# Which spectrum is copied: reordering one period of a four-layer kernel

## The chip, the cores and the metric

The kernel runs on one core of a Trainium2 chip. TensorE (PE) multiplies matrices into PSUM, VectorE (DVE), ScalarE (ACT) and GpSimd (POOL) do elementwise work, SyncE (SP) issues all DMAs. Each engine runs its own list of instructions in order and waits at semaphores. The metric is the device time of one execution in microseconds.

## The reference, cut to what matters

```
x = x + autocorrelation(layernorm(x), ctx, ctx)      # (32, 128, 1024), 8 heads
x = x + base(layernorm(x)) + experts(layernorm(x))   # 1024x1024 base, 8 LoRA experts, top 2
x = x + window_attention(layernorm(x), ctx)          # 8 heads, window 16
x = x + experts4(x)                                  # 4 LoRA experts, top 2

# autocorrelation, per batch, along the 128 rows of each of 1024 columns:
corr = ifft(fft(q) * conj(fft(k))).real ; k = v = ctx
w, idx = top_k(corr, 9) ; w = softmax(w)
out[t] = sum_i w_i * v[min(idx_i + t, 127)]
```

All of it is f32. The correlation is a product of two spectra. The transforms of 128 rows are products with tables of cosines and sines.

## The kernel before, in words

The 32 batches are independent. Each passes through three groups of stages: *a* (layer norm, spectra, correlation, top 9, softmax, aggregation by spectra, first residual), *b* (second norm, router, base product, experts, second residual, third norm, keys, values and queries) and *c* (window attention and last experts). Every engine runs a software pipeline: one step is one period, and in it up to four batches have their stages interleaved by hand in a function `step(i, live)`, where `live(lag)` says whether batch i - lag exists. All order is in these lists and in the semaphores; nothing is planned at run time. A full step has all stages.

PSUM is held by three tensors: `pa` (four banks of 512 f32; `pa_lo` is banks 0 and 1, `pa_hi` banks 2 and 3) for the a-stages and the projections of the context, `pb` (two) for the b-stages, `pc` (two) for the c-stages.

What the change touches, in the order of one period:
- `a_products` (L1105, DVE): four products of the weights' spectra with the context's long spectra `v_re`, `v_im`. Two of them read `pa_lo`, two `pa_hi`. `a_sum` (L1422 and L1424, POOL) adds them into `agg_re`, `agg_im`, one half of the columns after the other, four sums.
- `b_queries`: TensorE makes the attention's queries in `pb`, ACT writes their high half (L864), DVE the low half (L1149, output `sc`). `b_query_blocks` (L877 on ACT, L1450 on POOL) spreads the queries by head into `q_diag`, in two halves of eight blocks, six by ACT and two by POOL.
- `b_values(b, odd)` (L1169, DVE): transposes the values; SyncE then places them with four DMAs (L439, output `v_diag`).
- `gates` (L1180 to L1209, DVE): softmax and scaling of the experts. `c_mid` transposes the result (L696), `experts_mid` copies it on ACT, `c_delta` multiplies (L703, L704), `c_result` adds (L1261, DVE).
- `a_aggregate` (L561, L563): the inverse transform, in `pa` banks 0 and 1. `a_residual` (L1115, DVE) adds x, one half after the other, into `x_b`; `b_norm` (L1021) takes batch norm statistics of both halves; `variance` (L1025); POOL's `root` (L1395, L1400); `b_norm_rows` (L1038) writes the normalised rows `xn_b`, which `rows_to_features` (L575) transposes into `pb`.
- `a_context` (L495 to L497) transforms the next batch's context into `pa_lo`, `a_query` (L486) its query into `pa_hi`. `a_values` (ACT, L777) copies the context's spectrum from `pa_lo` to SBUF: first the two 64-row halves crosswise (real part to the imaginary rows) into `v_im`, then all into `v_re`. `a_product` (L1060, L1062, DVE) multiplies the query's spectrum in `pa_hi` with both. `a_corr` (L523, L524) transforms the products back, into banks 0 and 1. `a_context_long(b, n)` transforms the context in double length into `pa_hi`, real part (n = 0), then imaginary (n = 1), and `a_values_long` (ACT) copies these to `v_re` and `v_im`. The second waits for the first copy.
- `c_scores(b, g)` on PE (L649 to L657) makes one of four groups of attention scores in `pc`; on DVE `c_scores` takes their maximum (L1219) and `c_subtract` subtracts it (L1229). PE's next group waits for that subtraction. ACT's `c_exp` (L897), DVE's `c_sums` (L1236, L1238), POOL's `c_normalise` (L1458), ACT's `c_high` and POOL's `c_low` (L1431) follow.

The next period begins on PE with `b_router` (L591).

## Time and profile before

| | |
|---|---|
| time, median of 3 runs | 1823.69 us (1823.42 to 1826.07) |
| profiled execution | 1823.51 us, span 1821.7 us |
| busy, share of the span | PE 94%, DVE 86%, ACT 62%, POOL 50% |
| chain that ended last | PE 56%, DVE 20%, ACT 10%, POOL 8%, issue 5% |
| granted clock of PE, mean | 0.976 |
| one of ACT's query blocks (L877) | 710 ns, 384 of them |
| DMAs that place the values | 128 KB each, 5.0 us from issue to landing |

The clock is given as a share of full speed, 2.4 GHz. A busy PE is not a PE at its peak, since matmuls overlap in the pipeline and their ends are modelled: what a matmul costs is the distance between two starts. Idle time of an engine that is not the bottleneck costs nothing by itself.

### The profile page before, as it was taken

The numbers are of one execution on the slowest core, as the hardware profiler recorded it, in microseconds if no ns is written. First come the engines' busy times: TensorE is split into PE (matmuls) and PEld (weight loads), VectorE is DVE, ScalarE is ACT, GpSimd is POOL, SyncE is SP. The second block draws the span as 40 slices with busy tenths as digits, with TensorE's granted clock in tenths as the row PEclk, the third lists the DMA queues.
The fourth block names the chain that finished last, engine by engine and source line by source line (L and its number), as shares of the span: only waits on it lengthen the run. The fifth ranks groups of instructions, "written<-read, shape, count | busy, mean of one in ns | idle before, by whom it ended". The sixth has DMA issues, their size and how long they took to land.

```text
span 1821.7 us, 48202 instructions
## 1 busy us (share of the span) xinstructions
PE 1704.5 (94%) x19296; PEld 1081.3 (59%) x19296; DVE 1571.8 (86%) x4758; ACT 1131.7 (62%) x1929; POOL 903.1 (50%) x933
## 2 busy tenths in 40 slices
PE   4699999999999999999999999999999999999975
PEld 2356566666656666655666665666665666666553
DVE  7779889889889888988988898988898998889853
ACT  5257656666765666665666676566666666657642
POOL 2355554555554545555455555444555545555432
PEclk8899999999999999999999999999999999999995
DMA  6033322243332233332223343223443322333220
GB/s 225 24 59 71 59 53 51 52 71 71 71 59 48 50 58 71 71 66 48 51 50 71 71 71 59 50 50 55 71 71 71 47 49 50 69 71 59 31 30 24
DMA packets 549359, 111.37 MB, mean 61 GB/s; under 512 B 531088, under 2 KB 531344, under 8 KB 548624
## 3 DMA queue, kind: packets, MB, share of 16 engines
q1 hardware_dynamic: 549136, 108.30, 31.8%
q8 instruction: 152, 2.49, 0.6%
q14 instruction: 71, 0.58, 0.1%
HBM read 57.94 MB, written 16.78 MB: 41 GB/s over the span
## 4 chain that ended last, share of the span: by engine, by line
PE 56%; DVE 20%; ACT 10%; POOL 8%; issue 5%; DMA 0%; DVEq 0%; SPq 0%; POOLq 0%; ACTq 0%
PE pb L602 18%; PE pc L677 8%; ACT q_diag L877 6%; POOL prob L1424 4%; POOL rest L1422 4%; PE pa L523 4%; ACT v_im L777 3%; PE pa L495 3%; PE pa L524 3%; PE pa L496 3%; PE pa L497 3%; PE pb L591 3%; DVE rows_c L1251 2%; PE pa L563 2%; DVE rest L1105 2%
## 5 line engine op out<-in xcount | busy, mean ns | idle before, releaser
L602 PE MATMUL pb<-w_base_h,even_words 128*128 128x512 f16 x1024 | 324.8, 379 | 0.0
L1431 POOL TENSOR_TENSOR p_hl<-sc,p_hl 128x512 f16<-128x512 f32 x128 | 164.1, 1282 | 219.9 <-ACT p_hl L777 219.9
L1458 POOL TENSOR_TENSOR sc<-sc,sc_rec 128x512 f32<-128x512 f32 x128 | 134.4, 1050 | 266.2 <-DVE sc_rec L1238 266.2
L877 ACT ACTIVATE q_diag<-sc,own 128x512 f32<-128x512 f32 x384 | 244.3, 710 | 3.1 <-DVE sc L1149 3.1
L602 PE MATMUL pb<-w_base_l,even_words 128*128 128x512 f16 x512 | 193.9, 379 | 0.0
L486 PE MATMUL pa<-xn_a,tab 128*128 128x512 f32 x384 | 180.7, 607 | 3.8 <-ACT xn_a L777 3.8
L677 PEld LDWEIGHTS pc<-sc_t,v_diag 128*128 128x128 f16 x6144 | 170.2, 97 | 20.6 <-DVE sc_t L1245 5.9
L677 PE MATMUL pc<-sc_t,v_diag 128*128 128x32 f16 x6144 | 173.9, 177 | 5.5 <-DVE sc_t L1245 5.5
L655 PE MATMUL pc<-k_h,q_diag 128*128 128x32 f16 x2048 | 169.0, 177 | 0.0
L656 PE MATMUL pc<-k_l,q_diag 128*128 128x32 f16 x2048 | 168.4, 177 | 0.0
L657 PE MATMUL pc<-k_h,q_diag 128*128 128x32 f16 x2048 | 168.4, 177 | 0.0
L656 PEld LDWEIGHTS pc<-k_l,q_diag 128*128 128x128 f16 x2048 | 158.7, 97 | 15.8 <-issue 1.1
L602 PEld LDWEIGHTS pb<-w_base_h,even_words 128*128 128x128 f16 x1024 | 99.9, 98 | 113.7
L655 PEld LDWEIGHTS pc<-k_h,q_diag 128*128 128x128 f16 x2048 | 161.1, 97 | 7.9
L657 PEld LDWEIGHTS pc<-k_h,q_diag 128*128 128x128 f16 x2048 | 158.3, 97 | 0.0
L777 ACT ACTIVATE v_im<-pa 64x1024 f32<-64x1024 f32 (+1 forms) x96 | 98.1, 1021 | 95.8 <-PE pa L497 94.2
L777 ACT ACTIVATE rows_c<-pc 64x256 f32<-64x256 f32 x256 | 96.4, 376 | 95.1 <-PE pc L677 92.0
L1219 DVE TENSOR_REDUCE sc_max<-pc 128x16 f32<-128x512 f32 x128 | 84.5, 660 | 74.3 <-PE pc L657 74.3
L777 ACT ACTIVATE p_hl<-sc 128x512 f16<-128x512 f32 x128 | 100.7, 787 | 55.4 <-POOL sc L1458 51.0
L495 PE MATMUL pa<-ctx_hl,w_ctx_h 128*128 128x512 f16 x320 | 121.4, 379 | 12.5 <-POOL ctx_hl L1416 10.7
L1450 POOL TENSOR_TENSOR q_diag<-sc,own 128x512 f32<-128x512 f32 x128 | 129.2, 1042 | 5.5 <-DVE sc L1149 5.5
L1422 POOL TENSOR_TENSOR rest<-rest,v_im 128x512 f32<-128x512 f32 x64 | 81.8, 1279 | 90.8 <-DVE v_im L1105 90.8
(165 smaller groups left out, 4658.4 us busy)
## 6 DMA issues: line engine op xcount, KB each, us to landing
x_a<-in_x SPq DMA_DIRECT2D x32, 512.0 KB, 5.8
x_res<-in_ctx_in SPq DMA_DIRECT2D x32, 512.0 KB, 5.6
x_res<-in_x SPq DMA_DIRECT2D x32, 512.0 KB, 3.7
v_diag<-even_words SPq DMA_DIRECT2D x128, 128.0 KB, 4.9
v_diag<-p_hl SPq DMA_DIRECT2D x128, 128.0 KB, 5.0
out<-rows_c SPq DMA_DIRECT2D x32, 512.0 KB, 2.6
v_diag<-in_base_w SPq DMA_DIRECT2D x4, 1024.0 KB, 10.1
q_diag<-in_ra SPq DMA_DIRECT2D x1, 544.0 KB, 13.8
```

The costliest lines, as they stand in the source:

```text
L486: last = mm(place[:, n + h, :], lhsT, moving[:, h * HALF:(h + 1) * HALF], start=True, stop=True)
L495: mm(pa[:, n + h, :], w_ctx_h[:, table, :], high[:, cols], start=True, stop=False)
L602: mm(pb[:, h, :], rows[:, cols], weights[:, j, h * HALF:(h + 1) * HALF], start=(j == 0 and m == 0), stop=False)
L655: mm(place, q_halves[:, blk, :, HI], k_h[:, keys], start=False, stop=False)
L656: mm(place, q_halves[:, blk, :, HI], k_l[:, keys], start=False, stop=False)
L657: last = mm(place, q_halves[:, blk, :, LO], k_h[:, keys], start=False, stop=(i == GB - 1))
L677: last = mm(place, v_halves[:, blk % 2 * NBLK // 2 + blk // 2, :, v_part], p_halves[:, g % 2, i, :, p_part], start=(m == 0), stop=(m == 2))
L777: return nc.scalar.activation(dst, src, ACT.Copy)
L877: nc.scalar.activation(q_diag[:, blocks, head * QB:(head + 1) * QB], q_hl.rearrange("p (n t) -> p n t", t=QB)[:, blocks], ACT.Copy, scale= ...
L1422: g_.tensor_tensor(agg_re[:, cols], agg_re[:, cols], v_im[:, cols], ALU.add).then_inc(sum_w.sem, 1)
L1431: g_.tensor_tensor(part[:, :, :, LO], sc[:, g % 2, :, :], part[:, :, :, HI], ALU.subtract)\
L1458: g_.tensor_tensor(sc[:, g % 2, :, :], sc[:, g % 2, :, :], sc_rec[:, blocks].unsqueeze(2).to_broadcast([P, GB, KEYS]), ALU.mult)\
```

## The change

Of the two spectra that are multiplied, ACT now copies the query's (`a_query_crossed`, `a_query_same`), and DVE reads the context's from PSUM. The product comes out with the sign of its imaginary part turned, so one table changes its sign. PE makes the query's spectrum ahead of the aggregation, and the first long context directly behind the context, since `pa_hi` is free when ACT has copied it. The transposes of the second norm come before the first group of scores, and each half of the correlation comes behind a group of scores. On DVE the statistics of each half of the first residual directly follow that half (each waits for it), the product comes ahead of the first group's maximum and subtraction, and the queries' low half ahead of the values' second transpose. On ACT the copies move ahead of most query blocks.

```diff
-    corr_2 = np.concatenate([sin, -sin])
+    corr_2 = np.concatenate([-sin, sin])
@@ PE, a_context_long(b, 0)
-                    pe.wait_ge(prod_q.sem, prod_q.after(b))
-                    pe.wait_ge(prod_q2.sem, prod_q2.after(b))
+                    pe.wait_ge(v_out.sem, v_out.after(b))
@@ PE, step
                     c_router(i - 3)
+                if live(0):
+                    a_query(i)
                 if live(1):
                     a_aggregate(i - 1, 0)
...
                 if live(0):
                     a_context(i)
+                    a_context_long(i, 0)
+                if live(1):
+                    rows_to_features(i - 1, 0, 1, xn_b, pb)
                 if live(2):
                     c_scores(i - 2, 0)
                 if live(0):
-                    a_query(i)
-                if live(1):
-                    rows_to_features(i - 1, 0, 1, xn_b, pb)
+                    a_corr(i, 0)
                 if live(2):
                     c_scores(i - 2, 1)
                 if live(0):
-                    a_corr(i, 0)
-                    a_context_long(i, 0)
                     a_corr(i, 1)
@@ ACT
-            def a_values(b):
-                act.wait_ge(mm_ctx.sem, mm_ctx.after(b))
+            def a_query_crossed(b):
+                act.wait_ge(mm_q.sem, mm_q.after(b))
                 if not first(b):
                     act.wait_ge(sum_w.sem, sum_w.after(b - 1, 3))
                 for half in range(2):
...
-                    copy(v_im[rows, :], pa_lo[other, :]).then_inc(v_out.sem, 1)
+                    copy(v_im[rows, :], pa[other, 2:4, :].rearrange("p n t -> p (n t)")).then_inc(v_out.sem, 1)
+            def a_query_same(b):
+                act.wait_ge(mm_q.sem, mm_q.after(b))
                 if not first(b):
                     act.wait_ge(sum_w.sem, sum_w.after(b - 1))
-                copy(v_re[:, :], pa_lo).then_inc(v_out.sem, 1)
+                copy(v_re[:, :], pa_hi).then_inc(v_out.sem, 1)
@@ ACT, step
                     b_queries(i - 2)
-                if live(3):
-                    experts_exp(i - 3, 1, pc, E1)
-                if live(2):
                     b_query_blocks(i - 2, 0, 0)
                     b_query_blocks(i - 2, 5, 0)
+                if live(3):
+                    experts_exp(i - 3, 1, pc, E1)
+                if live(0):
+                    a_query_crossed(i)
+                if live(3):
+                    experts_mid(i - 3, 1)
+                if live(0):
+                    a_query_same(i)
+                if live(2):
                     b_query_blocks(i - 2, 1, 0)
-                if live(3):
-                    experts_mid(i - 3, 1)
...
-                if live(0):
-                    a_values(i)
@@ DVE, a_product
-                dve.wait_ge(mm_q.sem, mm_q.after(b))
+                dve.wait_ge(mm_ctx.sem, mm_ctx.after(b))
...
-                v.tensor_tensor(c2, pa_hi, v_im[:, :], ALU.mult).then_inc(prod_q2.sem, 1)
+                v.tensor_tensor(c2, pa_lo, v_im[:, :], ALU.mult).then_inc(prod_q2.sem, 1)
...
-                v.tensor_tensor(c1[:, :], pa_hi, v_re[:, :], ALU.mult).then_inc(prod_q.sem, 1)
+                v.tensor_tensor(c1[:, :], pa_lo, v_re[:, :], ALU.mult).then_inc(prod_q.sem, 1)
@@ DVE, a_residual, after each half
+                    dve.wait_ge(x1_out.sem, x1_out.after(b, h + 1))
+                    v.bn_stats(bn[1][:, h, :], x_b[:, cols]).then_inc(ln_bn[1].sem, 1)
@@ DVE, step
                 if live(1):
+                    b_queries(i - 1)
                     b_values(i - 1, 1)
-                    b_queries(i - 1)
                 if live(2):
                     gates(i - 2, 1, pc, E1)
                 if live(0):
                     a_residual(i)
+                    variance(i, 1)
                 if live(2):
                     c_result(i - 2, 0)
                 if live(0):
-                    b_norm(i, 1, x1_out)
-                    variance(i, 1)
-                if live(1):
-                    c_scores(i - 1, 0)
-                if live(0):
                     b_norm_rows(i, 1)
-                if live(1):
-                    c_subtract(i - 1, 0)
                 if live(-1):
                     a_product(i + 1)
+                if live(1):
+                    c_scores(i - 1, 0)
+                if live(1):
+                    c_subtract(i - 1, 0)
                 if live(2):
                     c_result(i - 2, 1)
```

## Rows read from the trace of the kernel before

**Rows 1.** Windows: busy us and (xrecords) per engine, clock, DMA share, GB/s.
```profile
754.90:808.60 53.70, 52.44 (x604) 33.41 (x603) 48.14 (x149) 34.88 (x61) 27.91 (x30) 1.00 0.34 60
```

**Rows 2.** Timeline of PE: start, length, engine, line, what, xcount, [idle before <-releaser].
```profile
796.12 3.60 PE L486 MATMUL pa<-xn_a,tab 128*128 128x512 f32 x8
...
804.81 1.07 PE L561 MATMUL pa<-rest,tab 128*128 128x512 f32 x2
...
808.77 0.22 PE L696 MATMUL pc<-ident_h,mid_hl 128*128 128x128 f16 x1
...
809.36 0.39 PE L703 MATMUL pc<-w_b_hh,mid_t 128*128 128x512 f16 x1 [0.37 <-ACT mid_t L777]
...
811.53 0.38 PE L649 MATMUL pc<-band_bf,ident_bf 128*128 128x512 bf16 x1
...
812.96 1.96 PE L486 MATMUL pa<-xn_a,tab 128*128 128x512 f32 x4
...
814.76 1.04 PE L575 MATMUL pb<-ident,xn_b 128*128 128x128 f32 x8
...
815.63 0.38 PE L649 MATMUL pc<-band_bf,ident_bf 128*128 128x512 bf16 x1
...
817.56 0.49 PE L523 MATMUL pa<-tab,xn_a 128*128 128x128 f32 x2 [0.35 <-DVE xn_a L1062]
...
823.96 0.38 PE L495 MATMUL pa<-ctx_hl,w_ctx_h 128*128 128x512 f16 x1
...
825.25 0.22 PE L591 MATMUL pb<-w_ra_h,even_words 128*128 128x136 f16 x1
```

**Rows 3.** Timeline of DVE, the same period.
```profile
803.75 1.24 DVE L1169 STREAM_TRANSPOSE p_hl<-v_pad 128x1024 f32<-128x1024 f32 x1
...
804.91 1.34 DVE L1149 SCALAR_TENSOR_TENSOR sc<-pb,bias_att,sc 128x1024 f16<-128x1024 f32 x1
...
806.14 0.14 DVE L1180 TENSOR_SCALAR small<-pc 128x4 f32<-128x4 f32 x1
...
808.22 1.45 DVE L1115 TENSOR_TENSOR x_b<-pa,x_res 128x512 f32<-128x512 f32 x2
...
811.04 1.28 DVE L1021 BATCH_NORM_STATS2 small<-x_b 128x6 f32<-128x512 f32 x2
...
812.36 0.20 DVE L1025 BATCH_NORM_AGGREGATE small<-small 128x2 f32<-128x12 f32 x1
...
813.76 0.80 DVE L1038 TENSOR_SCALAR xn_b<-x_b,small 128x1024 f32<-128x1024 f32 x1
...
819.39 0.63 DVE L1219 TENSOR_REDUCE sc_max<-pc 128x16 f32<-128x512 f32 x1
...
820.05 0.69 DVE L1229 TENSOR_TENSOR sc<-pc,sc_max 128x512 f32<-128x512 f32 x1
...
833.38 0.69 DVE L1219 TENSOR_REDUCE sc_max<-pc 128x16 f32<-128x512 f32 x1 [1.59 <-PE pc L657]
```

**Rows 4.** Timeline of ACT, POOL and the SyncE queue, the same period.
```profile
803.29 1.43 ACT L864 ACTIVATE sc<-pb,bias_att 128x1024 f16<-128x1024 f32 x1
...
805.01 5.74 SPq L439 DMA_DIRECT2D v_diag<-p_hl  x4
...
806.49 1.26 POOL L1424 TENSOR_TENSOR prob<-prob,v_re 128x512 f32<-128x512 f32 x1
...
812.92 0.55 POOL L1400 TENSOR_TENSOR small<-small 128x1 f32<-128x1 f32 x1
...
817.85 0.62 ACT L897 ACTIVATE sc<-sc 128x512 f32<-128x512 f32 x1
...
821.85 1.02 ACT L777 ACTIVATE v_re<-pa 128x1024 f32<-128x1024 f32 x1
```

**Rows 5.** Timeline, first batch and the end.
```profile
11.74 1.24 ACT L784 ACTIVATE xn_a<-x_a,small 128x1024 f32<-128x1024 f32 x1 [3.44 <-POOL small L1404]
...
1771.87 0.29 PE L696 MATMUL pc<-ident_h,mid_hl 128*128 128x128 f16 x1 [3.23 <-DVE mid_hl L1209]
```

More of the change, by code:

```diff
@@ L986, in step @@
                     b_queries(i - 2)
+                    b_query_blocks(i - 2, 0, 0)
+                    b_query_blocks(i - 2, 5, 0)
                 if live(3):
                     experts_exp(i - 3, 1, pc, E1)
-                if live(2):
-                    b_query_blocks(i - 2, 0, 0)
-                    b_query_blocks(i - 2, 5, 0)
-                    b_query_blocks(i - 2, 1, 0)
+                if live(0):
+                    a_query_crossed(i)
                 if live(3):
                     experts_mid(i - 3, 1)
+                if live(0):
+                    a_query_same(i)
                 if live(2):
+                    b_query_blocks(i - 2, 1, 0)
                     b_query_blocks(i - 2, 3, 0)
@@ L1001, in step @@
                     b_query_blocks(i - 2, 2, 1)
-                if live(0):
-                    a_values(i)
-                if live(2):
                     b_query_blocks(i - 2, 4, 1)
@@ L1115, in a_residual @@
                     v.tensor_tensor(x_b[:, cols], pa[:, h, :], x_res[:, cols], ALU.add).then_inc(x1_out.sem, 1)
-            def b_norm(b, n, before):
-                dve.wait_ge(before.sem, before.after(b))
-                layer_norm(b, n, x_b)
+                    dve.wait_ge(x1_out.sem, x1_out.after(b, h + 1))
+                    v.bn_stats(bn[1][:, h, :], x_b[:, cols]).then_inc(ln_bn[1].sem, 1)
             def b_norm_rows(b, n):
@@ L1340, in step @@
                 if live(0):
-                    b_norm(i, 1, x1_out)
-                    variance(i, 1)
+                    b_norm_rows(i, 1)
+                if live(-1):
+                    a_product(i + 1)
                 if live(1):
                     c_scores(i - 1, 0)
-                if live(0):
-                    b_norm_rows(i, 1)
                 if live(1):
                     c_subtract(i - 1, 0)
-                if live(-1):
-                    a_product(i + 1)
                 if live(2):
```

## The prediction, made before the changed kernel ran

> **What bounds the kernel now.** I read the windows first. In the steady stretch one period, that is one batch, takes 53.70 us and TensorE is busy for 52.44 of it, VectorE for 48.14, ScalarE for 34.88 and GpSimd for 27.91, with TensorE granted its full 2.4 GHz [rows 1]. So TensorE's order of work is the bound, and a change of order can give back only stalls. They are found by going through one period of its timeline and comparing start with start. A row's duration reaches about 0.17 us into the next row when nothing waits (814.76 + 1.04 against 815.63; so the eight f32 records from 796.12, 3.60 long, cost 3.43), so a gap of 0.35 before a row costs about 0.5. From the aggregation's first product (804.81) to the next period's router (825.25) are 20.44 us [rows 2], and the change reorders just this stretch. Three stalls lie in it:
> - the four aggregation products start at 804.81 and the next row at 808.77: 3.96 us, where eight such records cost 3.43. So 0.53 are waits for GpSimd's sums, the last of which ends at 807.75 [rows 2, 4];
> - 808.77 to 809.36, 0.59 us: transpose of the experts' rows, copy by ScalarE, products [rows 2];
> - the correlation starts at 817.56 with 0.35 idle in front of it, released by VectorE's second spectral product: about 0.5 us [rows 2].
>
> The other stalls (transposes of the last norm, the second router) lie ahead of 804.81, and the change leaves them as they are.
>
> **The change, part by part.** Times below are those of the period shown, with 804.81 as the fixed point.
>
> *TensorE.* The query's transform moves in front of the aggregation. It needs all four spectral products of the batch before, the last of which ended when the transpose behind it could start (803.75 [rows 3]), and its rows, made several us earlier. TensorE comes at 804.81: no wait. Now the sum of TensorE alone: query 1.80 (812.96 to 814.76), aggregation 3.43, transpose and copy 0.59, experts' products and context 2.17 (809.36 to 811.53), long context 1.29 (823.96 to 825.25), transposes 0.87 (814.76 to 815.63), scores 1.43 (811.53 to 812.96). That is 11.58, so the first half of the correlation is due at 816.39. The stretch 817.56 to 823.96 (6.40) holds two correlation halves, a long context and scores, so both halves take 6.40 - 1.29 - 1.43 = 3.68. Behind 816.39 come the two halves and two groups of scores, 3.68 + 2.86 = 6.54, which makes the second long context due at 822.93, and its 1.29 bring the next router to 824.22 [rows 2]. Against 825.25 that is 1.03 us less per batch, if nothing else waits. The two stalls that go are covered by the query (sums end 807.75, the aggregation's last product is due at 809.2) and by earlier products on VectorE. The 0.59 stays: transpose and copy remain neighbours.
>
> *VectorE.* This decides whether the due times hold. The low half of the queries now comes before the second transpose of the values. Its source is ScalarE's copy, which ends at 804.72 [rows 4], so VectorE, free at 803.84, stands still for 0.9 us that the transpose hid. I allow 0.05 for a hand-over between engines. Low half at 804.77 (lasts to the next start 1.23: 804.91 to 806.14), transpose at 806.00 (1.16: 803.75 to 804.91), gates at 807.16 [rows 3]. The gates take 2.08 to the first residual half, which I read as the residual's start 808.22 behind 806.14; that puts it at 809.24, against aggregation halves done by about 808.4 and 810.2. Then the halves: a statistics pair without a wait lasts 1.28 for two, 0.60 from start to start; with a wait on the instruction in front the next starts 0.03 after its end (819.39, 0.63 long, next 820.05) [rows 3]. So residual 809.24, statistics 809.96, residual 810.57, statistics 811.29, aggregate 812.01. The two new waits cost about 0.1 each on VectorE, some 6 us over 30 batches were they on TensorE's path. The Trainium skill has a rule here ("VectorE: DVE Perf Modes", section "The DRAIN you can't avoid"): a semaphore after each instruction adds nothing, since the pipe empties anyhow. The trace does not agree: 0.60 without a wait, 0.66 and more with one. By the rule everything from the aggregate on would come 0.2 earlier, the sum would stay what it is (the next lines show TensorE's own order as the later of the two), and only the chance of late hand-offs would shrink. I go by the rows.
>
> From the aggregate's start (812.36) to the end of GpSimd's root (813.47) are 1.11, and 0.06 more to the next start [rows 3, 4]. The norm of the rows therefore starts at 813.18 and ends at 813.98 (0.80). The transposes are due at 804.81 + 9.28 = 814.09: a margin of 0.1. From the norm's start (813.76) to the correlation's (817.56) were 3.80, with a subtraction of 0.67 between; without it 3.13. The correlation is released at 816.31 and due at 816.39, so this stall goes, by a margin of 0.1 again. The second residual half ends at 811.26, and the context products that wait for it are due at 804.81 + 1.80 + 3.43 + 0.59 + 0.88 = 811.51. The gates, done at 809.3, are in time for the experts' transpose at 810.04. Three margins of 0.1 to 0.2 in a row: this is where I may be wrong, and each 0.1 us lost costs 29 x 0.1 = 2.9 us.
>
> *ScalarE.* It copies the query's spectrum instead of the context's: three copies as before, at the 1.02 of the one at 821.85 [rows 4]. The first two now stand before the experts' copy: with the two query blocks (0.71 each) and the small exponential ahead they run from about 808.0 to 810.1; the experts' transpose ends at 810.2. Covered, by 0.1. Were they later, the experts' copy, the products, the context and the residual of the next group stand behind them. The third copy is done by 811.5, before the long context (due 812.8) that now waits for it instead of for the products. The query blocks come about 1.1 us behind their old time and the scores' start moves from 811.53 to 814.96, so they are covered.
>
> *What is late next.* The first scores end at 816.39. I allow 0.19 for the tail of 0.17 and the hand-over, so VectorE's maximum starts at 816.58; subtraction 0.66 later, done at 817.93; ScalarE's exponential at 817.98 against 817.85. From that exponential's start to the end of the copy of the long context (822.87) were 5.02 us of sums, normalising, splitting and copying [rows 4]. It ends at 823.00, TensorE starts at 823.05 and was due at 822.93: a new wait of 0.12. It had 1.1 us of slack before. The third scores need the second subtraction, done at about 821.2 and due at 821.5.
>
> *The moved DMAs.* The values' second transpose ends at 807.24 instead of 804.99, so SyncE's four placements, issued over 5.74 us from 805.01 [rows 4], start 2.3 later, and the load of the context and the store queue behind them. The last one is issued at 811.6 and at the page's 5.0 us lands at 816.6. The first that waits for it is ScalarE's feature copy right behind the exponential, at 818.5; TensorE wants the values at 825. Hidden, with 2 us left. The context load starts at 813, needed at 840.
>
> *Start and end.* In the first batch the query's rows are ready at 12.98, [rows 5]; until then TensorE made the context's transform, and ScalarE copied it during the query's. Now the query goes first and the context follows it: query at 13.0, slowly (at start 1.8 to 3.4 us), context to about 17.4, products to 19.8, long context before the correlation: between 0 and 2 us later, I take 1.2. At the end there is no a-part to hide behind: the gates come a transpose (1.24) later and the experts' transpose at 1771.87 already waited 3.23 for them [rows 5]: 0 to 2.5, I take 1.2.
>
> *Sum.* 1.03 - 0.12 = 0.91 us per batch. 29 steps have all stages: 26.4 us. Start and end give back 2.4. The profiled execution took 1823.51 us (span 1821.7), so 1823.5 - 26.4 + 2.4 = 1799.5. It lies 0.2 under the median of the runs, which changes nothing: 1800.
>
> **The rivals.**
> - *Late hand-offs.* One or more of the margins (norm before transposes, products before correlation, copies before the experts' copy) is missed by a total of 0.4 us. For: three margins near 0.1. Against: the period repeats to 0.02 us in the windows. It gives 1.03 - 0.52 = 0.5 per batch: 1823.5 - 14.5 + 2.4 = 1811.
> - *The gain comes back.* TensorE reaches the second long context early, but the chain of exponential, sums and copy is 0.9 later than I worked out, so that the wait there grows to the full gain. For: the copy is the last link of eight over four engines. Against: each link's time is in the trace. 1823.5 + 2.4 - 0 to 5: about 1823.
> - *VectorE becomes the bound: slower.* It is 0.46 late at the second subtraction (820.51 against 820.05) and TensorE wants its results 0.91 earlier. The only large idle time behind is 1.59 before the fourth maximum [rows 3], so 0.22 are left there; behind it the keys' low half has 0.5 more before TensorE waits. If VectorE is 0.75 us later than I have it, the gain shrinks one for one; from 0.75 + 0.91 = 1.66 on the kernel is slower. At 2.0: 29 x 0.34 + 2.4 = 12, so 1836. For: it is busy 90% and the change adds 0.9 idle and two waits. Against: the sum above leaves those 0.75.
> - *Everything fits and the ends cost nothing:* the whole 1.03 per batch is kept and start and end give nothing back: 1823.5 - 29.9 = 1794. If the query in its new place costs half of 3.43 and not 1.80, 2.6 less.
>
> **How the numbers follow.** Forecast 0.55 (1795 to 1806), late hand-offs 0.22 (1806 to 1818), gain comes back 0.07, slower 0.06, all fits 0.10. The range 1791 to 1816 leaves out the two bad cases, the end of the second and some of the last. A difference of 0.2%, 3.6 us, is about what the measurement can tell: faster than 1820 gets 0.87, within it 0.07, slower 0.06.
>
> **What would show it.** The period from batch to batch falls from 53.70 to about 52.8. The aggregation's products stand 3.43 apart in sum, with no wait for GpSimd. The 0.35 in front of the correlation is gone. VectorE shows a new idle of 0.9 before the queries' low half, released by ScalarE, and less than 0.5 instead of 1.59 before the fourth maximum. TensorE shows a new short wait for ScalarE's copy before the second long context. The 0.37 before the experts' products stays. I am wrong if the transposes wait for the norm by more than 0.2, if the experts' transpose or copy is late, or if the fourth maximum no longer waits for TensorE at all.

## The result, and the profile after

| | before | after |
|---|---|---|
| median of the runs, us | 1824.28 (4 runs) | 1809.38 (4 runs) |
| span of the profiled execution, us | 1821.7 | 1807.6 |
| one period in the steady stretch, us | 53.73 | 53.10 |
| TensorE's clock, mean | 0.976 | 0.975 |

The ratio of the times is 0.9918 (95% interval 0.9903 to 0.9933; brackets behind a ratio hold that interval from here on): faster, by 15 us, inside the range and 9 above the forecast of 1800. Most of what the prediction said is there: the two stalls are gone, the new wait is there at its size. But the period gained 0.63 and not 0.91, and the end cost more than it was given.

The page of the kernel after first, the chain that ended last:

```profile
PE 77%; DVE 15%; issue 4%; ACT 2%; POOL 1%; DMA 0%; DVEq 0%; SPq 0%; POOLq 0%; ACTq 0%
```

TensorE's busy time fell by 5 us only (1704.5 to 1699.1); it is waits that went. The chain runs over TensorE for 77% of the span, before for 56%.

One period of the kernel before, from one router's start to the next, and one of the kernel after, from one query transform to the next:

```profile
771.52:825.25 53.73, 52.47 (x604) 33.41 (x603) 48.17 (x149) 34.91 (x60) 27.94 (x29) 1.00 0.34 61
744.15:797.25 53.10, 52.28 (x606) 33.42 (x605) 48.47 (x149) 34.97 (x60) 27.91 (x30) 1.00 0.31 59
```

The 53.70 of [rows 1], which the prediction took for the period, was the length of a window, 0.03 short of a period. From start to start the kernel before has 53.73. A length taken between two starts of the same instruction does not have this fault.

TensorE's timeline of that period of the kernel after (answers to [rows 2]; a time of before less 60.66 is the same point here):

```profile
744.15 1.93 PE L486 MATMUL pa<-xn_a,tab 128*128 128x512 f32 x4
745.92 1.02 PE L560 MATMUL pa<-rest,tab 128*128 128x512 f32 x2
...
749.35 0.22 PE L695 MATMUL pc<-ident_h,mid_hl 128*128 128x128 f16 x1
749.94 0.39 PE L702 MATMUL pc<-w_b_hh,mid_t 128*128 128x512 f16 x1 [0.37 <-ACT mid_t L777]
...
750.81 0.38 PE L495 MATMUL pa<-ctx_hl,w_ctx_h 128*128 128x512 f16 x1
...
753.42 1.09 PE L574 MATMUL pb<-ident,xn_b 128*128 128x128 f32 x8
754.35 0.38 PE L648 MATMUL pc<-band_bf,ident_bf 128*128 128x512 bf16 x1
...
755.79 0.47 PE L523 MATMUL pa<-tab,xn_a 128*128 128x128 f32 x2
...
757.65 0.38 PE L648 MATMUL pc<-band_bf,ident_bf 128*128 128x512 bf16 x1
...
760.95 0.38 PE L648 MATMUL pc<-band_bf,ident_bf 128*128 128x512 bf16 x1
...
762.50 0.39 PE L495 MATMUL pa<-ctx_hl,w_ctx_h 128*128 128x512 f16 x1
...
763.95 0.23 PE L590 MATMUL pb<-w_ra_h,even_words 128*128 128x136 f16 x1
```

Read it start to start. The aggregation costs 749.35 - 745.92 = 3.43, the price of eight records without a wait. The correlation at 755.79 has nothing idle ahead of it. The experts' wait of 0.37 stands as it did. From the query to the router are 19.80 us; the prediction had 19.53, the kernel before 20.44 from its aggregation, which stood first there, to the router [rows 2]. These 0.64 are the whole gain of the period.

VectorE and ScalarE (answer to [rows 3, 4]):

```profile
744.10 1.38 DVE L1149 SCALAR_TENSOR_TENSOR sc<-pb,bias_att,sc 128x1024 f16<-128x1024 f32 x1 [0.92 <-ACT sc L867]
...
748.58 0.68 DVE L1118 TENSOR_TENSOR x_b<-pa,x_res 128x512 f32<-128x512 f32 x1
749.29 0.69 DVE L1120 BATCH_NORM_STATS2 small<-x_b 128x6 f32<-128x512 f32 x1
749.90 0.67 DVE L1118 TENSOR_TENSOR x_b<-pa,x_res 128x512 f32<-128x512 f32 x1
...
752.56 0.81 DVE L1041 TENSOR_SCALAR xn_b<-x_b,small 128x1024 f32<-128x1024 f32 x1 [0.45 <-POOL small L1398]
...
763.21 0.68 DVE L1133 TENSOR_TENSOR even_words<-pb,even_words 128x512 f16<-128x512 f32 x1
...
772.08 0.69 DVE L1219 TENSOR_REDUCE sc_max<-pc 128x16 f32<-128x512 f32 x1 [0.35 <-PE pc L656]
```

```profile
747.37 2.06 ACT L777 ACTIVATE v_im<-pa 64x1024 f32<-64x1024 f32 x2
749.61 0.28 ACT L777 ACTIVATE mid_t<-pc 128x128 f16<-128x128 f16 x1 [0.18 <-PE pc L695]
...
757.43 0.63 ACT L900 ACTIVATE sc<-sc 128x512 f32<-128x512 f32 x1 [0.51 <-DVE sc L1229]
```

The predicted times hold closely (predicted less 60.66 in brackets): queries' low half 744.10 (744.11), first residual 748.58 (748.58), norm 752.56 (752.52), exponential 757.43 (757.32). The last row of VectorE's fence but one is what the prediction did not look at: the low half of the features ends at 763.89, and the router starts 0.06 later. In the kernel before, the same work ended 1.3 ahead of the router at 825.25:

```profile
823.26 0.68 DVE L1133 TENSOR_TENSOR even_words<-pb,even_words 128x512 f16<-128x512 f32 x1
```

### The profile page after: what moved, and what is told of

Its sections match the earlier page's. It is cut to its first block, busy times and chain, and to the rows that moved or that the text cites. A ratio compares the mean times of both kernels' runs of the same rounds, so it can differ in the third digit from the quotient of the medians.

```text
span 1807.6 us, 48201 instructions
## 1 busy us (share of the span) xinstructions
PE 1699.1 (94%) x19296; PEld 1081.0 (60%) x19296; DVE 1581.0 (87%) x4758; ACT 1132.9 (63%) x1929; POOL 902.3 (50%) x933
## 4 chain that ended last, share of the span: by engine, by line
PE 77%; DVE 15%; issue 4%; ACT 2%; POOL 1%; DMA 0%; DVEq 0%; SPq 0%; POOLq 0%; ACTq 0%
PE pb L601 18%; PE pc L676 8%; PE pa L495 4%; PE pa L496 4%; PE pa L497 4%; PE pa L523 3%; PE pc L689 3%; PE pa L486 3%; PE pa L524 3%; PE pa L562 3%; PE pa L560 3%; PE pb L590 3%; PE pc L655 3%; PE pc L656 3%; PE pc L654 3%
## 5 line engine op out<-in xcount | busy, mean ns | idle before, releaser
L486 PEld LDWEIGHTS pa<-xn_a,tab 128*128 128x128 f32 x384 | 72.4, 196 | 105.9 <-issue 91.3
```

The costliest lines, as they stand in the source:

```text
L486: last = mm(place[:, n + h, :], lhsT, moving[:, h * HALF:(h + 1) * HALF], start=True, stop=True)
```

## Experiments

Each was run beside the kernel before; the medians are those of 4 runs, in experiment 3 of 5. An experiment without another word starts from the kernel after. Three dots in a diff stand for lines left out.

**1. Both halves of the features together.** Is it that row that holds the router?

```diff
                 if live(0):
                     b_features(i, 0)
+                    b_features(i, 1)
                 if live(-1):
                     a_top(i + 1, 0)
-                if live(0):
-                    b_features(i, 1)
```

> The changed kernel with one move on VectorE: the low part of the second half of the features comes directly behind the first half, ahead of the first group of top values. My theory (the router now waits for this low part, 0.16 us in each period, a wait that the prediction had missed): the router follows the long context after 1.29 instead of 1.45, period 52.94, 4 to 5 us less, about 1805. Rival (VectorE's lateness only shows there and is handed on to the next wait): the wait turns up before the attention products or the fourth maximum and the time stays at 1809.

1805.37 us, ratio 0.9895 [0.9881, 0.9908]. Its TensorE and VectorE:

```profile
760.76 0.39 PE L495 MATMUL pa<-ctx_hl,w_ctx_h 128*128 128x512 f16 x1
...
762.07 0.22 PE L590 MATMUL pb<-w_ra_h,even_words 128*128 128x136 f16 x1
```

```profile
758.87 1.28 DVE L1133 TENSOR_TENSOR even_words<-pb,even_words 128x512 f16<-128x512 f32 x2
```

The low half is done at 760.15, 1.9 ahead of the router, and the long context costs 1.31 instead of 1.45 (1.29 in the kernel before). The missed wait is worth 4.0 us of the kernel's time. The rival, by which VectorE's lateness would show up at the next wait and the time stay at 1809, falls.

**2. The values' transpose in its old place on VectorE.** Does the early low half of the queries, with its 0.92 of idle time, hold anything?

```diff
                 if live(1):
-                    b_queries(i - 1)
                     b_values(i - 1, 1)
+                    b_queries(i - 1)
```

> The changed kernel with one swap undone: on VectorE the values' second transpose again comes before the queries' low half. My theory (TensorE's own order is the later of the two up to the correlation): VectorE loses its new 0.92 us of idle, but the first residual half then waits for the aggregation, the norm comes only about 0.3 earlier, and the maximum behind it still waits for the first scores. Only the 0.06 in front of the transposes goes: period 53.0 to 53.1, time 1807 to 1810, at most 2 us under the changed kernel. Rival (VectorE's standstill of 0.92 is what is missing later at the router): the wait at the router goes as well, period 52.9, about 1804.

1807.82 us, ratio 0.9909 [0.9895, 0.9922]: 1.6 us less than after. Its runs lie between 1806.97 and 1809.52 and those of the kernel after between 1809.03 and 1809.99, so the time alone does not show the difference; the period does, with 53.02 for 53.10. The router's wait is unchanged (1.45 from long context to router). VectorE's wait has only moved, into the gates:

```profile
747.18 0.16 DVE L1192 SCALAR_TENSOR_TENSOR small<-small,pc 128x4 f32<-128x4 f32 x1 [0.91 <-ACT pc L887]
```

In the new place the queries are early enough for ScalarE's blocks; in the old one the gates wait 0.91 for the small exponential that ScalarE does behind those blocks. So the residual, at 748.31 with the query at 744.11, comes only 0.23 earlier. The transposes of the norm then cost 0.87, where they cost 0.93 in the kernel after. That 0.06 is the first of the three margins, used up: in the kernel after the norm ended at 753.37, and the transposes were due at 753.41.

**3. Statistics behind both halves of the residual.** What is the part with the statistics worth by itself?

```diff
-                    dve.wait_ge(x1_out.sem, x1_out.after(b, h + 1))
-                    v.bn_stats(bn[1][:, h, :], x_b[:, cols]).then_inc(ln_bn[1].sem, 1)
...
+                dve.wait_ge(x1_out.sem, x1_out.after(b))
+                layer_norm(b, 1, x_b)
```

> The changed kernel with the statistics again behind both halves of the residual. My theory (interleaving fills the wait for the second aggregation half): the aggregate comes 0.28 us later on VectorE, the transposes of the norm then wait 0.2 to 0.3 us, 29 times, and the time rises by 6 to 8 us to 1816. Rival (the two added waits cost what the place gains): no change, 1809.

1817.93 us, ratio 0.9965 [0.9952, 0.9979]: 8.6 us slower than after. Here the query starts at 747.63.

```profile
753.04 0.69 DVE L1118 TENSOR_TENSOR x_b<-pa,x_res 128x512 f32<-128x512 f32 x1 [0.30 <-PE pa L562]
...
756.30 0.81 DVE L1041 TENSOR_SCALAR xn_b<-x_b,small 128x1024 f32<-128x1024 f32 x1 [0.45 <-POOL small L1398]
```

The norm starts 8.67 behind the query, against 752.56 - 744.15 = 8.41, and TensorE takes 3.75 instead of 3.48 from the experts' first product to the transposes: 0.27 for 0.26, one for one. With statistics between the halves, VectorE works in the time in which it now waits 0.30 for the aggregation. Nothing was left of the margin of 0.1 in the prediction, or a part of the 0.26 would have cost nothing.

**4. The query ahead of the aggregation, nothing else** (from the kernel before). Is TensorE's order enough?

```diff
                 if live(0):
-                    a_query(i)
...
+                if live(0):
+                    a_query(i)
                 if live(1):
                     a_aggregate(i - 1, 0)
```

> The kernel before with only the query's transform moved ahead of the aggregation on TensorE. ScalarE still copies the context's spectrum late and VectorE multiplies late. My theory (the correlation's start was tied to the chain of ScalarE's copies and the products): the 0.53 us of waits in the aggregation go, but TensorE then stands 0.9 instead of 0.35 us before the correlation; the period stays 53.7, time 1822 to 1826. Rival (each stall is TensorE's own, so that covering one is a gain): 29 x 0.53 = 15 us less, 1808.

1870.73 us, ratio 1.0252 [1.0238, 1.0266]. Neither theory had it: 1822 to 1826 was expected. TensorE of one period, whose query starts at 774.93:

```profile
780.13 0.22 PE L696 MATMUL pc<-ident_h,mid_hl 128*128 128x128 f16 x1
...
785.98 1.09 PE L575 MATMUL pb<-ident,xn_b 128*128 128x128 f32 x8 [1.50 <-DVE xn_b L1038]
...
788.92 0.49 PE L523 MATMUL pa<-tab,xn_a 128*128 128x128 f32 x2 [0.43 <-DVE xn_a L1062]
```

The aggregation's waits do go: 780.13 - 774.93 = 5.20, the query and eight records. But the query's old place had hidden the norm: the scores in front of the transposes take 3.09 instead of 1.43. The period is 54.97, so 29 of them cost 36 of the 46 us. Of the rest, 9 us were lost by the second router (135.84, in the kernel before 126.67), and no run names their cause. I read this first as a matter of the norm's lateness, and tested that twice.

**5. The same, with the norm of the rows ahead of the maximum on VectorE.**

```diff
                 if live(0):
                     b_norm(i, 1, x1_out)
                     variance(i, 1)
-                if live(1):
-                    c_scores(i - 1, 0)
                 if live(0):
                     b_norm_rows(i, 1)
+                if live(1):
+                    c_scores(i - 1, 0)
```

> The kernel before with the query's transform ahead of the aggregation, and on VectorE the norm of the rows ahead of the first scores' maximum. With the query moved alone the time rose by 46 us: TensorE came to the transposes 1.8 us earlier, while the norm waited behind a maximum that waits for the first scores, and 1.5 us of idle opened there. My theory: that queue on VectorE is the whole loss, and with the norm first the correlation is tied to ScalarE's copies and the products as before, so the period returns to 53.6 to 53.8 and the time to 1820 to 1827, no gain. Rival (with both covers the aggregation's 0.53 us is gained at last): 1808. Second rival (the norm is late for other reasons too): above 1835.

1932.50 us, ratio 1.0589 [1.0574, 1.0605]. VectorE of one period, then two windows inside that period, then two whole periods from router to router, then TensorE:

```profile
807.33 0.81 DVE L1038 TENSOR_SCALAR xn_b<-x_b,small 128x1024 f32<-128x1024 f32 x1 [1.01 <-POOL small L1400]
```

```profile
808.00:810.00 2.00, 1.57 (x11) 1.07 (x12) 1.97 (x4) 1.98 (x3) 1.78 (x1) 0.85 0.38 154
810.00:812.00 2.00, 1.63 (x50) 1.52 (x49) 2.00 (x3) 2.00 (x4) 0.59 (x1) 0.50 0.00 0
```

```profile
650.70:708.60 57.90, 54.91 (x604) 35.52 (x603) 48.40 (x150) 34.92 (x60) 27.93 (x29) 0.94 0.31 56
708.60:764.04 55.44, 52.40 (x605) 33.61 (x604) 47.53 (x146) 34.80 (x60) 27.10 (x29) 1.00 0.33 58
```

```profile
808.19 1.09 PE L575 MATMUL pb<-ident,xn_b 128*128 128x128 f32 x8 [1.33 <-DVE xn_b L1038]
...
811.78 0.80 PE L523 MATMUL pa<-tab,xn_a 128*128 128x128 f32 x2 [0.37 <-DVE xn_a L1062]
...
815.36 0.63 PE L495 MATMUL pa<-ctx_hl,w_ctx_h 128*128 128x512 f16 x1
```

The wait for the norm is nearly as long as in experiment 4 (1.33 for 1.50). VectorE now stands still 1.01 for the root: the statistics start only at 804.80, behind the experts' result, and that waits 0.77 for its products. So the order of norm and maximum was not what held it; what is left is the place of the statistics, which experiment 6 moves.

The 62 us on top of experiment 4 have two parts. The smaller is order: VectorE's products now stand behind norm, maximum and subtraction, and the correlation comes 811.78 - 802.53 = 9.25 behind the experts' transpose, 0.46 later than in experiment 4 (8.79). In a period whose clock stays at 1.00 that is all: 55.44 against 54.97, or some 13 us in 29 periods. The larger is the clock granted to TensorE. It falls to 0.50, its lower level of 1.2 GHz, at about 809.4, behind the wait of 1.33 us and within that of 0.24, and stays there until 816; the wait of 0.37 already lies in the slow stretch. Half a correlation costs 815.36 - 811.78 = 3.58 where it costs 1.89 in experiment 4, in which the clock was 1.00 from 784 to 792. Of the 29 full periods 22 have such a stretch and are 57.6 to 57.9 us long; the other 7 have 55.4. So these stretches cost 2.1 to 2.5 us each, some 50 us in all, and the mean clock is 0.938 against 0.971.

**6. The same as 4, with the statistics ahead of the experts' result, and the norm ahead of the maximum.** This gives VectorE the order of the kernel after from the residual to the norm of the rows; its two spectral products stay behind maximum and subtraction, and ScalarE's order is as before.

```diff
                     v.tensor_tensor(x_b[:, cols], pa[:, h, :], x_res[:, cols], ALU.add).then_inc(x1_out.sem, 1)
+                    dve.wait_ge(x1_out.sem, x1_out.after(b, h + 1))
+                    v.bn_stats(bn[1][:, h, :], x_b[:, cols]).then_inc(ln_bn[1].sem, 1)
...
                 if live(0):
                     a_residual(i)
+                    variance(i, 1)
                 if live(2):
                     c_result(i - 2, 0)
-                if live(0):
-                    b_norm(i, 1, x1_out)
-                    variance(i, 1)
...
```

> The kernel before with the query's transform ahead of the aggregation and VectorE's order taken from the changed kernel for the norm: statistics behind each residual half, aggregate ahead of the experts' result, norm ahead of the maximum. ScalarE still copies the context's spectrum behind nine query blocks. In the two runs before this, the norm came 5.7 to 5.9 us behind the aggregation, because the statistics stood behind the experts' result, which waits for its products; in the changed kernel it is 4.1. My theory: with the statistics ahead, the wait before the transposes goes, and what is left is the correlation tied to the late copies: 0.9 us or more of idle before it, period 53.5 to 53.9, time 1818 to 1828, no gain over the kernel before. Rival (the late copies do not matter, the order does): 1808 to 1812, as the changed kernel.

1876.64 us, ratio 1.0286 [1.0271, 1.0301]. It was expected near the kernel before and is some 50 us slower. Its TensorE and ScalarE, with the query starting at 778.03:

```profile
783.24 0.22 PE L696 MATMUL pc<-ident_h,mid_hl 128*128 128x128 f16 x1
...
792.03 0.49 PE L523 MATMUL pa<-tab,xn_a 128*128 128x128 f32 x2 [1.35 <-DVE xn_a L1062]
```

```profile
783.67 3.78 ACT L877 ACTIVATE q_diag<-sc,own 128x512 f32<-128x512 f32 x6
787.47 2.06 ACT L777 ACTIVATE v_im<-pa 64x1024 f32<-64x1024 f32 x2
```

The norm is no longer waited for: it ends at 786.92, and the transposes start at 787.43, behind the scores. The correlation is, and it starts exactly where it did: 792.03 - 783.24 = 8.79 behind the experts' transpose. In experiment 4 it is 788.92 - 780.13 = 8.79, in the kernel before 817.56 - 808.77 = 8.79 [rows 2]. This is one chain, and it begins on ScalarE: copy of the experts' rows, six query blocks, then the copies of the spectrum (787.47 behind 783.67 + 3.78), VectorE's two products, correlation. VectorE's first product starts 0.09 behind the end of ScalarE's second copy in all three kernels, and here it stood idle for 0.59 before that. Whatever is put ahead of the experts' transpose on TensorE moves the correlation by as much: the query brings 1.24 (5.20 against 3.96), and the period was 1.24 longer (54.97 against 53.73). My theory of a late norm falls. What holds experiments 4 and 6 back is that the copies stand behind the experts' copy and six blocks on ScalarE. In the kernel after, where the query's spectrum is copied instead of the context's, the correlation comes 755.79 - 749.35 = 6.44 behind the experts' transpose and waits for nothing. A rival was not run: copies of the context's spectrum ahead of the six query blocks, which could shorten the chain without the swap of the spectra.

The 6 us by which this kernel is slower than experiment 4 are not in the chain, since the usual period is the same. They go with the clock: five of its 29 full periods hold a short stretch at 0.50 and last 56.6 us; in experiment 4 four do, and last 55.5.

**7. The query behind the aggregation, with the query's spectrum still the one copied**, and on ScalarE the experts' copy first, since the query now comes close ahead of it.

```diff
                 if live(1):
                     a_aggregate(i - 1, 0)
                     a_aggregate(i - 1, 1)
+                if live(0):
+                    a_query(i)
...
+                if live(3):
+                    experts_mid(i - 3, 1)
                 if live(0):
                     a_query_crossed(i)
-                if live(3):
-                    experts_mid(i - 3, 1)
-                if live(0):
                     a_query_same(i)
```

> The changed kernel with only the query's transform put behind the aggregation, ahead of the experts' transpose, and on ScalarE the experts' copy ahead of the query's copies, so that it isn't held up. My theory: the query's place ahead of the aggregation is needed above all for ScalarE: its three copies now end at about 814.1 on the scale of the prediction, the first long context waits 0.8 us for them, and the 0.53 in the aggregation is back: period 54.3 to 54.5, time 1843 to 1852. Rival (only the cover of the aggregation is lost): 0.5 us per period, 1825.

1866.45 us, ratio 1.0229 [1.0212, 1.0246]. ScalarE's query blocks, then a row of the table of waits of TensorE (total, times, longest) and its timeline:

```profile
776.46 6.22 ACT L880 ACTIVATE q_diag<-sc,own 128x512 f32<-128x512 f32 x10
```

```profile
PE pa L495 <- ACT v_re L777: 40.8, 62, 1.9
```

```profile
776.61 0.39 PE L495 MATMUL pa<-ctx_hl,w_ctx_h 128*128 128x512 f16 x1 [0.80 <-ACT v_re L777]
...
787.65 0.39 PE L495 MATMUL pa<-ctx_hl,w_ctx_h 128*128 128x512 f16 x1 [0.39 <-ACT v_re L777]
```

1843 to 1852 was expected. The first wait is what was expected: the long context writes where the query's spectrum is still being read. The 0.54 of the aggregation is back too (767.21 to 771.18 for eight records). The second wait was not expected. ScalarE has ten query blocks to do behind the copies, and its exponential starts at 782.58, when they end, with no idle time; in the kernel after it waited 0.51 for VectorE. So the copy of the long context comes late too, twice per period in all (62 times). The two parts of the change need each other: with the new copies but the query late the kernel is 57 us slower than after, with the query early but the old copies (experiment 4) 61.

**8. Features together, and ScalarE's copy of the long context ahead of the normalised probabilities' copy.** Is the predicted wait of 0.12 that copy?

```diff
+                if live(1):
+                    a_values_long(i - 1, 0)
                 if live(3):
                     c_high(i - 3, 0)
                     c_exp(i - 3, 1)
                 if live(1):
-                    a_values_long(i - 1, 0)
                     a_values_long(i - 1, 1)
```

> The changed kernel with the low part of the features moved up as in the run before (1805.4), and on ScalarE the copy of the long context's real part ahead of the first group's split, where ScalarE was idle for 1.25 us. My theory: the 0.11 us that the scores' stretch is longer in front of the second long context is the wait for this copy, and goes: period 52.83, 29 x 0.11 = 3 us less, 1802. Rival (VectorE's low features or top values take over at once): 1805.

1801.77 us, ratio 0.9873 [0.9857, 0.9890]: 3.6 less than experiment 1.

```profile
759.86 0.38 PE L495 MATMUL pa<-ctx_hl,w_ctx_h 128*128 128x512 f16 x1
```

The scores ahead of the second long context cost 1.44 again; in the kernel after they cost 762.50 - 760.95 = 1.55. It was that copy.

**9. The old order in the last steps only**, where there is no next batch: on VectorE the values' transpose ahead of the queries and the maximum ahead of the norm, on TensorE the scores ahead of the norm's transposes.

```diff
                 if live(1):
-                    b_queries(i - 1)
+                    if live(-1):
+                        b_queries(i - 1)
                     b_values(i - 1, 1)
+                    if not live(-1):
+                        b_queries(i - 1)
...
```

> The changed kernel with the old order in the last steps only, where no next batch hides anything: values before queries and maximum before norm on VectorE, first scores before the transposes on TensorE. All full periods are as in the changed kernel. My theory (the end gives back 3.9 us of the 18.0 gained by the last full period): 3 to 4 us less, 1805.5. Rival (these stalls at the end lie beside a longer chain): 1809.

1807.34 us, ratio 0.9905 [0.9890, 0.9920]: 2.0 less than after, where 3 to 4 were expected. The last experts' transpose but one stands at 1757.89 in the kernel after and at 1756.11 here (the row of the kernel after answers to [rows 5]). In both, TensorE makes the queries' product ahead of it, four records; after first, then here:

```profile
1757.89 0.29 PE L695 MATMUL pc<-ident_h,mid_hl 128*128 128x128 f16 x1 [4.57 <-DVE mid_hl L1209]
```

```profile
1746.78 3.00 PE L486 MATMUL pb<-xn_b,w_att 128*128 128x512 f32 x4 [3.16 <-DVE xn_b L1041]
```

```profile
1746.44 1.98 PE L486 MATMUL pb<-xn_b,w_att 128*128 128x512 f32 x4 [3.16 <-DVE xn_b L1043]
```

Of the 1.8 us between the two transposes the larger part is not the order. The clock was 0.50 from 1747.6 to 1751.0 in the kernel after and 1.00 here, behind the same wait of 3.16; so ScalarE's copy of the queries starts 5.08 behind the product there (1751.86) and 3.98 here (1750.42), which is 1.1. From that copy to the experts' transpose are 6.03 there and 5.69 here: the transpose's old place is worth 0.3. The other 0.3 were there at the product; with the 0.14 by which this kernel was behind at the end of the last full step, the old order of the norm gave 0.5. So the order gave back 0.8 us, and the clock happened to give 1.1. Whether the order had a part in the clock was not tried.

**10. All together**: experiments 1, 2, 8 and 9, and the one stall that the change had left. The experts' transpose goes ahead of the aggregation's last product, which then covers the copy, and ScalarE does its first query blocks behind the copies.

```diff
                 if live(1):
-                    a_aggregate(i - 1, 0)
-                    a_aggregate(i - 1, 1)
+                    a_aggregate(i - 1, 0, 0)
+                    a_aggregate(i - 1, 0, 1)
+                    a_aggregate(i - 1, 1, 0)
                 if live(3):
                     c_mid(i - 3)
+                if live(1):
+                    a_aggregate(i - 1, 1, 1)
+                if live(3):
                     c_delta(i - 3)
...
```

> Everything that helped in one kernel (features together, copy ahead, old order at the end, values before queries in every step), and the last stall of the stretch attacked: the experts' transpose goes ahead of the last aggregation product, so that ScalarE's copy runs beside that product; on ScalarE the two query blocks go behind the copies. My theory: of the 0.59 us between transpose and products 0.3 to 0.5 are gained in each of 29 periods on top of the rest, 1802 - 4 - 9 to 14 = 1784 to 1789. Rival (the query blocks, now behind the copies, make the first scores late): about 1798 and a wait for ScalarE before the scores.

1792.64 us, ratio 0.9824 [0.9810, 0.9839]: the fastest of the study, 17 us ahead of the change as made, with a period of 52.60. 1784 to 1789 was expected.

```profile
795.76 0.22 PE L696 MATMUL pc<-ident_h,mid_hl 128*128 128x128 f16 x1
796.73 0.38 PE L703 MATMUL pc<-w_b_hh,mid_t 128*128 128x512 f16 x1
...
797.77 0.38 PE L495 MATMUL pa<-ctx_hl,w_ctx_h 128*128 128x512 f16 x1
```

```profile
796.93 0.69 DVE L1127 TENSOR_TENSOR x_b<-pa,x_res 128x512 f32<-128x512 f32 x1 [0.31 <-PE pa L563]
```

The wait of 0.37 is gone, transpose and last product cost 0.97 together. But the aggregation now ends nearer to the context, so the second residual half, which ends at 797.62, is waited for: the experts' four products take 1.04 up to the context instead of 0.87, and the transposes of the norm come 0.1 late. From the experts' transpose to the next scores it is 5.64 (743.16 to 748.80, one period earlier) where the kernel after takes 5.86 for the same work (754.35 - 749.35 and the 0.86 of a product): 0.22 gained of the 0.3 to 0.5 expected. That is the larger part of why it ended above what was expected.

## Why the prediction was right, and where it was off

*The two stalls.* Right as stated. Aggregation 3.43, no idle time ahead of the correlation, as far as records show it.

*The three margins of 0.1.* Two held: VectorE's second product (754.42, 1.22 long) ended at 755.64 and the correlation started at 755.79, its due time; ScalarE's copies ended at 749.43, and its experts' copy waited for TensorE, not TensorE for it. The first, norm before transposes, was used up: the norm ended only 0.05 ahead of the transposes, and they lost 0.06 by it (experiment 2). Experiment 3 shows the price of more: 0.26 of lateness cost 0.27 per batch, 8.6 us.

*Two new waits on VectorE.* From start to start, 748.58 to 749.29 is 0.71 with a wait and 749.29 to 749.90 is 0.61 without. So the wait costs 0.10, as taken. By a measurement in the Trainium skill ("VectorE: DVE Perf Modes", section "The DRAIN you can't avoid"), eight copies with and without semaphores in the same time, it would cost nothing; this trace does not agree. The same section says that a next instruction that is not held back starts earlier, and with that the 0.61 does agree.

*The new wait of 0.12.* Right: 0.11, and experiment 8 removed it.

*What failed: "the next router".* The sum brought the router 1.03 earlier and asked of the last link only whether the copy was in time. It did not ask what else the router reads. VectorE's low half of the features stands behind the first search of the next batch, and this work did not move when TensorE did. It cost 0.14 to 0.16 per batch, 4.0 us in all (experiment 1). The other 0.1 of the 0.27 missing between query and router is 0.06 at the transposes and 0.04 in the two correlation halves (1.86 each, 3.72 against the 3.68 that I had as a difference of other rows). The second half now stands behind scores and not behind a context, and behind scores the first record pair of a half costs 0.30 (755.79 to 756.09, 759.09 to 759.39), behind the context of the kernel before 0.22 (820.75 to 820.97).

*The sum of the steady part.* The lead over the kernel before, router against router, is 0.25 us at the second router (126.42 against 126.67), where the full steps begin, and 18.0 at the router behind the last full step (1667.02 against 1685.02). So the 29 full periods gained 17.8 where the prediction had 26.4. That is 29 times 0.63, less 0.7 in two periods that were 53.4 and 53.5 long; what those two waited for was not looked into.

*Start.* Mis-sized, by an amount that one execution hardly shows. The first correlation starts at 21.36 instead of 18.09, and at the first router the loss is 1.2 us (81.2 against 80.0), as priced; but the next step, which is not full, gave 1.4 back, and the sum had nothing for it. The first router stands between 79.9 and 82.2 in experiments 1, 2, 3, 8, 9 and 10, whose order up to the first correlation is that of the kernel after, so the agreement with 1.2 may well be luck.

*End.* Mis-sized: 3.9 us lost, 1.2 given. From 18.0 the lead falls to 16.2 at the queries' product (1746.78 against 1762.98) and to 14.0 at the last experts' transpose but one (1757.89 against 1771.87). The first 1.8 are lost in the last step with a second norm, where the scores no longer stand between norm and transposes, which wait 3.07 for it (before, 1.59). But the old order gives back only 0.5 of them: in experiment 9 the first scores of that step wait 1.90 for VectorE's experts' result, where the kernel before waits 0.88 for a query block. Of the next 2.2, 1.1 are the lower clock behind the queries' product, which the prediction had no term for and the kernel before did not have there (its four records took 1.98), and 1.1 are the gates, a transpose later, close to the 1.24 in the prediction. With the 0.3 at the gates the old order gave back 0.8 of all this (experiment 9); the rest is read from the trace and no run shows it by itself.

In sum: 0.25 + 17.8 - 3.9 = 14.1, the difference of the two spans, where the prediction had 24. The 10 us between them are 8.7 that the steady part gave less and 2.7 that the end cost more, less 1.4 by which the start went better than priced.

*The rivals.* "Late hand-offs" gave 1811 and came nearest in time, yet of its three margins only one was missed, by 0.06 where it had a total of 0.4; most of the loss came from a fourth place that it did not name. That it came nearest is luck. VectorE did not become the bound: the fourth maximum still waits 0.35 for TensorE, where "less than 0.5" was said and the kernel before had 1.59 [rows 3]. The slower ending did exist near this change, but by another mechanism: the chain over ScalarE of experiments 4 and 6.

## What to carry to other kernels

When an order of work is moved earlier, list for each later start on the bounding engine every operand it reads, not only the one that was latest before; the wait that takes the gain is one that had slack. Find chains by equal spacing: an interval that is the same to 0.01 us in three kernels (here 8.79) points to one chain, and the traces name its first link, where to cut. Take a period from start to start of one instruction, not from the ends of a window. At the end of a loop, cover is gone; an order that pays in the steady part may want its old form there, though here that was worth only about 0.8 us.

## What was not expected of the hardware

TensorE's granted clock mostly stayed at 1.00 through waits of 1.50 and 0.43 us per period (experiment 4): 25 of the 29 full periods have no lower stretch, and the four that have one are 0.6 us longer. Where waits of 1.33 and 0.24 us stood ahead of the correlation (experiment 5) it fell to 0.50 in 22 of 29, for nearly 7 us each, and each such stretch cost 2.1 to 2.5 us, most of it in one half of the correlation, which took 1.7 us longer. So the sum of waits alone does not give the time of such a kernel: with the wait of 0.37 behind the fall, experiment 5 had 1.94 us of them in this stretch and experiment 4 had 1.93, and experiment 5 took 62 us more, some 50 of them with the clock. What exactly tips the clock was not tried. At the end of the kernels the same wait of 3.16 us was followed by 0.50 in one kernel and by 1.00 in two (experiment 9), which moved the time by 1.1 us; a difference of 1 or 2 us between two such kernels should be looked for there before it is put down to their order.
